# Keys of two groups sent in pieces, two output pairs summed on TensorE, half a gram product and eight tail tiles in a two-layer attention and mixture-of-experts kernel

## What is computed

```python
xn = layernorm(x)
x = x + causal_attention(xn, 16 heads of 16) @ w_o + experts(xn, 16 experts, top 2 by sigmoid + bias)
xn = layernorm(x)
# linear attention, sequence-wide: norms over all tokens, one product per feature
qkv = xn @ W + b;  q, k, v = split(qkv)
qn, kn = q / norm(q, over tokens), k / norm(k, over tokens)
a = qn * sum(kn * v, over tokens)
# 16 experts, top 4 by softmax, and a shared expert
moe = sum over top 4 of w * (silu(xn @ we1) * (xn @ we3)) @ we2
shared = (silu(xn @ ws1) * (xn @ ws3)) @ ws2
out = x + a + shared / 5 + moe * 4 / 5
```

## Time and profile before

| | us |
|---|---|
| median of 3 runs | 903.83 |
| lowest and highest | 898.98, 904.56 |
| the profiled execution | 906.89 |
| its span, first to last instruction | 905.2 |

### The profile page before, as it was taken

One profiled execution on the slowest core, in us unless ns is written; L12 is line 12 of the kernel. 1 busy time (PEld: TensorE's weight loads), 2 busy tenths in 40 slices (PEclk: granted clock), 3 DMA queues, 4 the chain that ended last, 5 costly groups with the idle time before them and its releaser, 6 DMA issues. The chain is left out here.

```text
span 905.2 us, 16683 instructions
## 1 busy us (share of the span) xinstructions
PE 830.5 (92%) x4934; PEld 449.4 (50%) x4935; DVE 645.3 (71%) x1472; ACT 468.8 (52%) x883; POOL 437.1 (48%) x720
## 2 busy tenths in 40 slices
PE   5978699999988999999999998989999989999993
PEld 3533133334533444444444432138644769888982
DVE  5587988898867888888788888437547336555648
ACT  2643154556654666666565666754313046555547
POOL 3422045603652433653435446531578848878820
PEclk9997698999998999999999999989999989999997
DMA  9654772210272121272211222325852235555566
GB/s 328 212 129 137 207 142 89 89 46 25 81 128 71 49 61 56 80 127 71 70 38 38 55 60 76 93 65 188 302 166 88 88 117 164 157 154 159 158 255 246
DMA packets 70182, 110.05 MB, mean 122 GB/s; under 512 B 16662, under 2 KB 49942, under 8 KB 69590
## 3 DMA queue, kind: packets, MB, share of 16 engines
q1 hardware_dynamic: 49430, 54.04, 22.9%
q0 software_dynamic: 16000, 45.70, 14.7%
q10 hardware_dynamic: 4672, 9.34, 3.4%
HBM read 62.53 MB, written 46.22 MB: 120 GB/s over the span
## 5 line engine op out<-in xcount | busy, mean ns | idle before, releaser
L1275 DVE TENSOR_REDUCE part_max<-ps_row 128x1 f32<-128x512 f32 (+3 forms) x560 | 353.6, 670 | 71.1 <-PE ps_row L1429 38.7
L1139 ACT ACTIVATE probs<-ps_st 128x1024 f32<-128x1024 f32 (+3 forms) x320 | 278.2, 896 | 204.6 <-PE ps_st L1408 188.2
L1333 PE MATMUL ps_o<-probs,v_all 128*17 128x512 f32 (+3 forms) x1280 | 150.4, 542 | 6.9 <-POOL probs L1009 5.6
L1429 PE MATMUL ps_row<-ks,qs 96*128 96x512 bf16 (+3 forms) x320 | 110.2, 379 | 13.7 <-DVE part_max L1275 9.3
L1429 PE MATMUL ps_row<-xt_ks,qs 96*128 96x512 bf16 (+3 forms) x320 | 104.5, 354 | 6.9 <-DVE part_max L1275 6.5
L1682 POOL DMA_INDIRECT yd<-moe_ys,moe_home x79 | 82.6, 1046 | 25.5 <-POOL moe_home L1676 13.4
L1408 PE MATMUL ps_st<-qs,ks 99*128 99x512 bf16 (+3 forms) x320 | 88.7, 360 | 2.9 <-DMA qs<-max_parts 2.7
L1408 PE MATMUL ps_st<-qs,xt_ks 99*128 99x512 bf16 (+3 forms) x320 | 85.7, 356 | 3.9 <-ACT probs L1139 2.8
L1702 PE MATMUL moe_ps_h<-moe_xs_t,moe_w_now 128*128 128x128 f32 x632 | 86.0, 280 | 1.3 <-ACT moe_xs_t L1607 0.8
L1702 PEld LDWEIGHTS moe_ps_h<-moe_xs_t,moe_w_now 128*128 128x128 f32 x632 | 78.4, 195 | 3.2 <-DVE moe_w_now L1569 2.0
L1429 PEld LDWEIGHTS ps_row<-ks,qs 96*128 96x128 bf16 x320 | 31.9, 100 | 95.6 <-DVE part_max L1275 52.8
(11 more groups left out here) (288 smaller groups left out, 1307.3 us busy)
## 6 DMA issues: line engine op xcount, KB each, us to landing
moe_xs<-xd SPq DMA_DIRECT2D x79, 129.0 KB
qk_parts<-probs SPq DMA_DIRECT2D x16, 384.0 KB, 4.2
qs<-qk_parts SPq DMA_DIRECT2D x96, 64.0 KB, 2.5
moe_xs<-xd POOLq DMA_DIRECT2D x47, 128.0 KB, 2.4
yd<-moe_ys POOLq DMA_DIRECT2D x47, 128.0 KB, 2.1
xd<-zeros POOLq DMA_DIRECT2D x2, 2048.0 KB, 15.5
moe_w<-in_w ACTq DMA_DIRECT2D x2, 2048.0 KB
w<-in_we SPq DMA_DIRECT2D x8, 512.0 KB
```

Of the source, the lines that this page charges most:

```text
L1139: act.activation(probs[:, at % NPB, :, off:CH], ps_st[at % 2][:, :, off:CH], ACT.Exp, scale=HD ** -0.5).then_inc(exp_done, 1)
L1275: dve.tensor_reduce(part_max[reduced % 2][:, h:h + k, i, j:j + 1], bank[:, 0:k * w].rearrange("p (h w) -> p h w", h=k), AX_X, ALU.max).the ...
L1333: mm = pe.matmul(ps_o[32 * q:32 * q + HD + 1, off:CH], m.v_all[:, k, g * HG + q, :], probs[:, (at + q // 2) % NPB, q % 2, off:CH], start=F ...
L1429: mm = pe.matmul(cols, qs[c][0:KROWS, h, i * P:(i + 1) * P], ks[g % 2][0:KROWS, h, j * CH:j * CH + w], start=True, stop=(j < c))
```

## The change

- `load_keys` takes the bands to send. For groups 2 and 3 SP no longer sends six at the `turn`: it notes them, and sends band t at the first `exp` of the plan that is at least 3 t exponentials later. Group 1 is sent as before. For group 2 the bands stand at exponentials 91, 93, 96, 99, 102 and 105: two ahead of the first `gather`, three between it and `return`, the last behind `return`.
- `add_gram` makes of the second bank only columns 128 to 256 (the matrix is symmetric). PE turns the missing block from the first bank's copy, ACT copies it, and the products with `w` start with k = 1.
- `TAIL_FIRST` = 8: a fourth tail pair in the second stage, in `ps_o`.
- In the last part pairs 2 and 3 are summed by PE: it multiplies each scaled result by five times the identity (`five`, made by POOL at the stage's start) into the pair's bank, and DVE adds a fifth of the bank. For the other six pairs ACT scales three of four results, and DVE adds these and takes the fourth with a multiply by a weight and add, one instruction for each tile. Loads, additions and PE's work go in three orders written out by hand.

The diff, with little context:

```diff
@@ -331,9 +331,9 @@
-def load_keys(eng, m, g, tokens, done):
-
-    for t in range(TERMS):
+def load_keys(eng, m, g, tokens, done, terms=range(TERMS)):
+
+    for t in terms:
         src = m.qk_parts[K_PART[t], D + g * HG * HD:D + (g + 1) * HG * HD, tokens]
@@ -672,6 +672,7 @@
+KEY_SPACE = 3
 SHARE_STEPS = (("gather", 3), ("invert", 13), ("return", 14), ("spread", 17), ("share", 28))
@@ -886,9 +887,14 @@
                          m.ones16[0:PARTS, :].unsqueeze(1).to_broadcast([PARTS, HG * T, P])).then_inc(ones_in[1], 16)
-            n = 0
+            n, at, pieces = 0, 0, []
             for u in plan:
-                if u[0] == "pv" and ends_pair(u[1]):
+                if u[0] == "exp":
+                    at += 1
+                    while pieces and pieces[0][0] <= at:
+                        _, g, t = pieces.pop(0)
+                        load_keys(sp, m, g, slice(0, S), k_in[g % 2], [t])
+                elif u[0] == "pv" and ends_pair(u[1]):
@@ -912,11 +918,12 @@
                     n += 1
-                    if g + 1 < NG and c == (1 if g == 0 else 2):
-
-                        if g >= 1:
-                            sp.wait_ge(pv_done, last_pv(g - 1, C - 1))
-                        load_keys(sp, m, g + 1, slice(0, S), k_in[(g + 1) % 2])
+                    if (g, c) == (0, 1):
+                        load_keys(sp, m, 1, slice(0, S), k_in[1])
+                    if g + 1 < NG and g >= 1 and c == 2:
+
+                        sp.wait_ge(pv_done, last_pv(g - 1, C - 1))
+                        pieces += [(at + KEY_SPACE * t, g + 1, t) for t in range(TERMS)]
                     if (g, c) == (1, 0):
@@ -1539,10 +1546,12 @@
         tail_done, finished = l.sem("moe1_tail_done"), l.sem("moe1_finished")
-        scaled = l.sem("moe1_scaled")
+        scaled, five_ready = l.sem("moe1_scaled"), l.sem("moe1_five_ready")
+        five = l.sb("moe1_five", [P, P])
         yg_pair = [yg8[:, 2 * n:2 * n + 2, :, :] for n in range(T // 4)] + [
...
         step_sem = l.sem("moe1_dve")
+        by_act = [(n, k) for n in LAST_LOADS for k in range(top if n in SUMMED else top - 1)]
         block = ctx.enter_context(nc.Block())
@@ -1587,10 +1596,10 @@
                 sp.wait_ge(y_out[b], 16 * len(range(b, tiles, U)))
-            for n in range(T // 2):
+            for n in LAST_LOADS:
                 sp.dma_start(yg[2 * n], rows_of(2 * n)).then_inc(fetched[n], 16)
-            for n in range(T // 2):
-                sp.wait_ge(finished, n + 1)
+            for at, n in enumerate(LAST_ADDS):
+                sp.wait_ge(finished, at + 1)
                 sp.dma_start(out[0, 2 * n * P:2 * (n + 1) * P, :].rearrange("(i p) d -> p i d", p=P),
@@ -1617,11 +1626,11 @@
                 act.wait_ge(y_out[b], 16 * len(range(b, tiles, U)))
-            for n in range(T // 2):
+            for n in LAST_LOADS:
                 act.dma_start(yg[2 * n + 1], rows_of(2 * n + 1)).then_inc(fetched[n], 16)
-            for n in range(T // 2):
+            for n in LAST_LOADS:
                 act.wait_ge(fetched[n], 32)
-                for k in range(top):
+                for k in (k for pair, k in by_act if pair == n):
                     for i in (2 * n, 2 * n + 1):
@@ -1653,20 +1662,27 @@
             step = Steps(dve, step_sem)
-            for n in range(T // 2):
+            for n in LAST_ADDS:
                 both = m.x[:, 2 * n:2 * n + 2, :]
-                for k in range(top):
-                    dve.wait_ge(scaled, n * top + k + 1)
-                    step.then(dve.tensor_tensor(both, yg_pair[n][:, :, k, :], both, ALU.add))
-                if 2 * n < TAIL_FIRST:
-                    dve.sem_inc(finished, 1)
-                else:
-                    dve.wait_ge(tail_done, n + 1 - TAIL_FIRST // 2)
+                if n not in SUMMED:
+                    for k in range(top - 1):
+                        dve.wait_ge(scaled, by_act.index((n, k)) + 1)
+                        step.then(dve.tensor_tensor(both, yg_pair[n][:, :, k, :], both, ALU.add))
+                    dve.wait_ge(fetched[n], 32)
+                    for i in (2 * n, 2 * n + 1):
+                        step(dve.scalar_tensor_tensor(m.x[:, i, :], yg[i][:, top - 1, :], m.r["weight"][:, i, top - 1:top],
+                                                      m.x[:, i, :], ALU.mult, ALU.add))
+                    step.sync()
+                if n in LAST_TAILS:
+                    dve.wait_ge(tail_done, LAST_TAILS.index(n) + 1)
                     dve.scalar_tensor_tensor(both, ps_tail[n].rearrange("p (i d) -> p i d", d=D), 1.0 / (TOP1 + 1), both,
                                              ALU.mult, ALU.add).then_inc(finished, 1)
+                else:
+                    dve.sem_inc(finished, 1)
...
         def _(pool):
+            pool.tensor_scalar(five[:, :], m.ident[:, :], float(TOP1 + 1), None, ALU.mult).then_inc(five_ready, 1)
             step = Steps(pool, pool_sem)
@@ -1715,15 +1731,27 @@
             pe.wait_ge(hid_ready, tiles)
-            for n in range(TAIL_FIRST // 2, T // 2):
+            pe.wait_ge(five_ready, 1)
+            for n in LAST_TAILS:
+                bank = ps_tail[n]
                 if n == T // 2 - 2:
...
                 for i in (2 * n, 2 * n + 1):
-                    mm = shared_tail(pe, m, ps_tail[n], i)
+                    if n not in SUMMED:
+                        mm = shared_tail(pe, m, bank, i)
+                        continue
+                    for k in range(top):
+                        pe.wait_ge(scaled, by_act.index((n, k)) + 1)
+                        mm = pe.matmul(bank[:, i % 2 * D:(i % 2 + 1) * D], five[:, :], yg[i][:, k, :],
+                                       start=(k == 0), stop=(k == top - 1))
                 mm.then_inc(tail_done, 1)
...
-TAIL_FIRST, TAIL_BEFORE = 6, 14
+TAIL_FIRST, TAIL_BEFORE = 8, 14
+SUMMED = (2, 3)
+LAST_LOADS = (0, 1, 2, 4, 5, 3, 6, 7)
+LAST_ADDS = (0, 1, 4, 2, 5, 6, 3, 7)
+LAST_TAILS = (4, 5, 6, 2, 7, 3)
 ROOT_BEFORE = 7
@@ -1756,11 +1784,11 @@
         banks_g = [l.ps(f"ps_gram{b}", [P, CH]) for b in range(KH)]
-        ps_g = [b[:, 0:DP] for b in banks_g]
+        ps_g = [b[:, k * P:DP] for k, b in enumerate(banks_g)]
         bank_l = l.ps("ps_l2", [P, CH])
...
         ps_o = l.ps("ps_o2", [P, 2, D])
-        ps_tail = [banks_g[1], banks_g[0], bank_l]
+        ps_tail = [banks_g[1][:, :], banks_g[0][:, :], bank_l[:, :], ps_o[:, :, :].rearrange("p i d -> p (i d)")]
         ps_gw, ps_sums, ps_ones = banks_g, bank_l, banks_g[0]
@@ -1881,7 +1909,9 @@
             for k in range(KH):
-                act.copy(gram[:, k, :], ps_g[k]).then_inc(gram_copied, 1)
+                act.copy(gram[:, k, k * P:DP], ps_g[k]).then_inc(gram_copied, 1)
+            act.wait_ge(gram_done, 2)
+            act.copy(gram[:, 1, 0:P], banks_g[0][:, 0:P]).then_inc(xt_ready, 1)
             act.wait_ge(logit_ready, 1)
@@ -1999,8 +2029,8 @@
                 dve.wait_ge(b_in, 16)
-                for k in range(KH):
-                    dve.wait_ge(gw_done, k + 1)
+                for k in (1, 0):
+                    dve.wait_ge(gw_done, KH - k)
                     step(dve.tensor_tensor(prod[:, k, 0:2 * D], ps_gw[k][:, :], w[:, k, 0:2 * D], ALU.mult))
@@ -2080,7 +2110,7 @@
                 pair = m.x[:, 2 * b:2 * b + 2, :]
-                step(dve.scalar_tensor_tensor(pair, bank[:, :].rearrange("p (i d) -> p i d", d=D), 1.0 / (TOP1 + 1), pair,
+                step(dve.scalar_tensor_tensor(pair, bank.rearrange("p (i d) -> p i d", d=D), 1.0 / (TOP1 + 1), pair,
                                               ALU.mult, ALU.add))
@@ -2115,7 +2145,7 @@
                     for k in range(KH):
-                        mm = pe.matmul(ps_g[k], xn[:, i, k * P:(k + 1) * P], xn[:, i, 0:DP],
+                        mm = pe.matmul(ps_g[k], xn[:, i, k * P:(k + 1) * P], xn[:, i, k * P:DP],
                                        start=(i == 0), stop=(i == T - 1))
@@ -2186,7 +2216,10 @@
             pe.wait_ge(gram_copied, KH)
-            for k in range(KH):
+            pe.transpose(banks_g[0][:, 0:P], gram[:, 0, P:2 * P], m.ident[:, :]).then_inc(gram_done, 1)
+            for k in (1, 0):
+                if k == 0:
+                    pe.wait_ge(xt_ready, T + 1)
                 for j in range(KH):
```

## The result

In a first series of 18 executions each, the changed kernel took 0.9882 of the time of before (95% interval 0.9851 to 0.9913). Nine of its 18, the profiled one among them (938.57 us), ran in a slower state of the chip and are left out of that ratio. On two more chips, with the kernel before at 896.75 and 896.17 us, the whole change took 885.77 us (0.9880, 0.9842 to 0.9918) and 886.34 us (0.9882, 0.9848 to 0.9915). On the 903.83 of the prediction 0.9882 is 893.2, against the 893.4 predicted. The parts did not add up as predicted, which is what the experiments are about. The trace read here is that of the first of these two chips (885.77 us median; the profiled execution took 886.03, its span 884.3).

A forecast was written before the change was run, and what follows sets the result against it. PE, busy 92% of the span, stood at 268 us for the divisors' gather; SP after POOL ended the second stage, DVE the last part. -8.4 + 0 + 0 - 2.0 = -10.4 from 903.83 gave 893.4 us, range 888 to 900.

The forecast's parts named there:

- Keys in pieces: PE's stop at 268 us: four key pieces fewer ahead of the divisors' gather, -8.4 us, bounds -2 and -8.4.
- The landing (264.9): The divisors' gather, leaving at about 258.2 us, should land at 264.9, before DVE reaches `invert`.
- PE is busy without a break behind this place, so the whole schedule moves up: Behind PE's stop at 268 us: why the time gained there counts in full, 8.4 us.
- the 5.8 and 2.6 predicted: At `invert`: 5.8 us from PE's shorter stop, 2.6 us from the half clock behind it.
- The gram product: Second stage, line 2118: 64 records stay, taking about 12 us; 1.9 us of PE's work saved, alone worth nothing.
- this half does not move POOL's chain: Second stage: DVE's first chunk of slots, which starts POOL's dispatch, was held by a transfer, not by PE.
- The stage boundary: Second stage's end: PE's end moves +3.5 us against 2.6 of slack; taken as 0, net bounds -2.2 to +2.8.
- If the clock holds: Start of the experts' stage: full clock after PE's shorter stop returns 2.2 us; net -1.3, else +0.9.
- Rival (b): Second stage's end: waits swallow the gram saving and the clock falls all the same, 2.8 us, 896.2; chance 0.12.
- The last part: Last eight pairs: DVE's work 23.0 us against 26.2, DVE ends at 900.6 instead of 902.6, -2.0 us.
- Rival (c): Last part: PE's sums run at half clock, +6.1 to +6.5 us instead of -2.0, 901.7; chance 0.06.
- Rival (d): Group two: last key pieces, behind SP's wait for `invert`, come too late; PE stops, 905 and more; chance 0.04.

The follow-up runs named there:

- four_ahead: Only the keys in pieces, but four of the third group's bands ahead of the gather instead of two: 890.61 us, 0.9936 of the kernel before.
- before_2: The kernel before, unchanged, run and profiled once more: 896.17 us, 1.0001 of before.
- before: The unchanged kernel in its first profile: that execution took 906.89 us, the median of the three runs was 903.83 us.
- keys_gram: Keys in pieces and half gram product, six tail tiles and the last part of before, against the kernel before: 883.93 us, 0.9870.
- keys_only: Only the keys of groups 2 and 3 in pieces, all else as in the kernel before: 885.93 us, 0.9875 of it.
- again: The whole change run once more for a clean trace, against the kernel before at 896.75 us: 885.77 us, 0.9880.
- keys_stage2: The whole change with the last part of before (new keys, half gram product, eight tail tiles), against the kernel before: 882.5 us, 0.9874.
- no_keys: All of the change but the keys in pieces, against the kernel before at 896.75 us: 893.26 us, 0.9957.
- stage2_only: Only the half gram product and eight tail tiles, last part of before, against the kernel before at 896.75 us: 895.15 us, 0.9981.
- again_2: The whole change once more on another chip, with its own profile, against the kernel before at 896.17 us: 886.34 us, 0.9882.
- no_sums: The whole change without PE's sums, DVE adding all eight pairs, in plain orders, against the kernel before at 896.17 us: 888.0 us, 0.9903.

## Why the prediction was right or wrong

**Keys in pieces: mechanism right, size probably too small.** Predicted 8.4, measured 11.2 alone (0.9875) and 893.26 - 885.77 = 7.5 on top of the rest; the four kernels with the new keys and the old last part agree on the larger figure (0.9870 to 0.9879, `four_ahead` left out). The landing (264.9), DVE's coming (267.16 predicted, 267.87) and PE's full clock to 290 us came as worked out. The term that came out too small is "PE is busy without a break behind this place, so the whole schedule moves up". From `invert` to the second stage's first instruction it took 321.9 to 322.1 us in six of the nine traces with the keys moved, 324.7 in `before_2` and 326.1 to 329.7 in the other three without. The 2.7 of `before_2` are the half clock right behind the stop. The rest of the others is mainly a second stretch of half clock, at 566 to 574 us, some 4 us long and so worth 2, at the end of the attention where PE is busy two thirds of 12 us. It stood in three of the four traces without the new keys and, at 558 to 566 and twice as long, in two of nine with them; `before` has a third one at 590. On average the traces with a freed gather reach `invert` at 267.7 and the second stage at 590.4, those without the new keys at 274.0 and 600.7: 6.3 and another 4.0 us, against the 5.8 and 2.6 predicted. Whether the keys' new place makes it rarer, or chance did, these few traces do not tell. Nor do they bear on the fourth group's bands, which no run moved by themselves.

**The gram product: right.** 64 records, 12.1 us against about 12. That it alone is worth nothing holds in time (`keys_gram`), within the interval. Its reason, "this half does not move POOL's chain", holds for the start of the dispatch, 21.3 us into the stage in `keys_gram` as in `keys_only`. It sits badly with the dispatch's length, shorter in five traces of eight with the half product and in none of five without; that the half product causes this isn't shown.

**The stage boundary: the 0 was right, its working only half.** The mis-sized term is PE's chain, which moved by 2.6 us against the 3.5 predicted (DVE's last product ended 125.1 us into the stage in `before_2` and 127.7 in the whole change). The experts' stage began 128.3 and 128.2 us into the stage: not 0.9 later but at the same distance, because GpSimd's dispatch ended sooner: the slack of 2.6 us that the sum held it against was no constant. "If the clock holds" was left open, and it is open in fact: behind the short stop it held in three traces of six (last section). Rival (b), 2.8 us lost, is half seen: in `again` the clock fell all the same, but the 2.8 us show in no trace, and in time `keys_stage2` (0.9874) speaks against them without excluding them.

**The last part: right.** 2.0 predicted; 1.9 between `no_keys` and `stage2_only`, 1.7 to 2.2 in the traces. From PE's first tail to DVE's end it took 37.0 us against the "some 36" of the prediction and 38.1 before. On top of the keys this gain is in the traces, but the medians, whole change against keys alone, don't show it: it is smaller than their intervals. The traces of `again` and `keys_only` show what stood against it there: the last part is 1.8 us shorter, and the second stage 1.6 longer, by the half clock at its start. Rival (c) falls: PE's sums of pair 2 ran at full clock in `again`, mostly at half in `again_2`, and nothing was later for it:

```profile
862.00:864.00 2.00, 1.79 (x6) 0.60 (x4) 0.21 (x1) 2.00 (x7) 0.00 (x0) 1.00 1.04 418
864.00:866.00 2.00, 1.91 (x9) 1.70 (x10) 0.96 (x2) 2.00 (x7) 0.00 (x0) 1.00 1.02 404
```

```profile
862.00:864.00 2.00, 1.90 (x6) 0.92 (x5) 0.29 (x1) 2.00 (x6) 0.00 (x0) 0.69 1.03 410
864.00:866.00 2.00, 2.00 (x6) 1.55 (x5) 0.88 (x2) 2.00 (x6) 0.00 (x0) 0.50 1.03 408
```

(`again` first, `again_2` second; the last part took 32.0 and 31.7 us.)

**Rival (d)** falls too: SP was free of its wait for `invert` at 268.24, the last band left at 268.62, and PE's matmuls had no wait up to 320 us.

So the sum hit the time, 0.9882 against 893.4 / 903.83 = 0.9885, and that it hit so closely is luck: one term is 3 us too small by the keys' own run, and the last part's 2 us, seen in the traces, are not seen on top of it in the times.

## What to carry to other kernels

When a small transfer whose landing an engine waits for is issued behind large ones from the same queue, count the large ones ahead of it: here each of 256 KB cost it 2.2 us, and six right behind it cost the kernel nothing. Move it ahead; splitting and spreading is needed only as far as it does that. Once a stage is ended by two chains of nearly one length, an edit to either gives little, and a trace should be read for both ends before more work is moved into it.

## What the runs showed of the hardware

Stretches of half clock come and go: between executions of one program (`again_2` has one at 862 us that `again` lacks), and between kernels whose code up to that point is the same. The second stage begins alike in `again` and in `keys_stage2`, and the granted clock from 590 to 592 us is not the same; `again` first:

```profile
590.00:592.00 2.00, 1.96 (x5) 1.63 (x6) 0.26 (x3) 0.00 (x0) 0.12 (x1) 0.50 0.17 39
```

```profile
590.00:592.00 2.00, 2.00 (x11) 1.64 (x10) 1.18 (x3) 0.00 (x0) 0.00 (x0) 1.00 0.29 51
```

Where the clock fell there, the first slots were ready 21.8 to 22.0 us into the stage, elsewhere 20.2 to 20.4: 1.6 us. It fell there in five traces of thirteen, both of the whole change among them. At the start of the experts' stage it fell behind each of the seven stops of 4.0 to 4.3 us. Behind the six short ones, of 1.3 to 1.9 us, which the eighth tile brings, it fell in `again`, `again_2` and `no_sums` and held in `keys_stage2`, `no_keys` and `stage2_only`. Where it held, the stage took 120.3 to 120.6 us from the first to the last turn of a row tile, where it fell 121.9 to 122.9 (first profile of before left out): some 2 us. Both traces of the whole change fell, so chance from one execution to the next and something in the kernel can't be told apart here. The stop in `keys_stage2` is that of `again` (1.34, above), and the clock is not:

```profile
715.57 0.63 PE L1701 MATMUL moe_ps_x<-ident,moe_xs 128*128 128x128 f32 x4 [1.35 <-PEq L1741]
...
717.00:719.00 2.00, 2.00 (x19) 2.00 (x19) 0.54 (x2) 1.14 (x4) 0.21 (x1) 1.00 0.54 132
```

The executions of the whole change spread from 880.4 to 891.3 us with the mean granted clock from 0.975 to 0.963 or so. The Trainium skill ("TensorE: Matmul & The Clock Gate", "HAM oscillation — how this bites in real kernels") describes pauses of 3 to 5 us between bursts of matmuls after which the clock is down every time. The seven long stops agree. The short ones, of 1.3 to 1.9 us, had both outcomes, and the pauses of PE's sums, 1.3 us and less, don't bear on what it describes.

The other page named in the prediction, the Trainium skill's "DMA: Bandwidth & Descriptors" ("Queues, rings and completion order"), says that completion is not first-in, first-out for one issuing engine. No overtaking shows in `again`, where the landings from 261 to 271 us stand in the order of issue. That transfers never overtake isn't shown by it.
